# Sorted expert batches of 256 rows, and router logits taken from feature-major data before the normalisation

## The chip, the cores and the metric

The program runs on one core of one Trainium2 chip. The metric is the time on the device in microseconds (us), from the start to the end of one execution, as the median of several. Engines are named as the profile does: PE is TensorE (PEld its weight loads), DVE VectorE, ACT ScalarE, POOL GpSimd, and SP SyncE, which here only issues DMAs.

## The reference, cut to what matters

A graph layer of 3327 nodes with 128 features (attention with three heads over a dense adjacency, two GRU cells) is followed by a mixture of 8 experts of which each node takes two. The part that the change touches:

```python
# x: (3327, 128) result of the graph layer; D = 128, E = 8, K = 2, H = 256
mu = mean(x); var = mean(square(x - mu))
xn = (x - mu) * rsqrt(var + EPS) * gamma + beta       # of an x normalised once before
logits = einsum('bsd,de->bse', xn, Wr) + br
top_vals, top_idx = top_k(logits, 2);  w = softmax(top_vals)
for e in range(8):
    h = gelu(xn @ W1[e] + b1[e])                      # 128 -> 256
    y = y + (h @ W2[e] + b2[e]) * w_full[..., e]      # 256 -> 128
return x + y
```

The graph layer's own last step is `x + de * edge_output + dn * node_output`, with de and dn the diagonal of the adjacency (the same for both).

## The kernel before

Nodes are padded to NP = 3328 = 26 tiles of 128. There are seven chunks of columns, the first of 256 nodes and six of 512. The program has four stages in order of time.

**Graph stage.** Masks, scores and the sum over neighbours for three heads (L1729 on PE, L1242 and L1251 on DVE). The change leaves it alone.

**GRU loop.** One pass for each chunk c. The engines run their own programs and meet by semaphores. PE: `edge(c)` (12 instructions of 512 columns; a matmul of 32-bit floats is two instructions), `attend(c)` (8), `turn_nodes(c-1)` (four transposes), `node(c)` (10). ACT does the gates' sigmoids and tanh, and `attention_kept`. DVE does `candidate` and `mix` for the edge cell, then `nodes_kept(c-1)` (adds the GRU result into `x_kept`, node-major, and takes its statistics), then `candidate` and `mix` for the node cell; the last instruction of the pass raises `dve_mixed`. `temporary(c, 3)` holds the GRU result, feature-major.

Into this loop the dispatch of nodes to experts is woven. The seven chunks make four sets, `SETS = ((0, 1), (2, 3), (4, 5), (6,))`; `due(c, ago)` names the set whose last chunk came `ago` passes earlier. For set g, with the pass in which it runs:

- `deviations(g)` on DVE, ago 1: mean and inverse deviation, 20 small dependent instructions; then `rows_normed(g)` on ACT writes the normalised rows twice (`rows_out`).
- `turn_back(g, k)` on PE and `rows_back(g, k)` on ACT, ago 2: transposes the normalised rows and applies gamma and beta.
- `logits(g)` on PE (L1837, 8 columns for each tile) and `route(g)` on DVE (L1388 to L1406: two maxima, their one-hot forms, running counts), ago 3; `weigh(g)` on ACT; `ranks(g)` on PE (L1845 to L1850), which waits for `route(g)` and stands in PE's program in front of the next `edge`.
- `place(g)` on DVE (L1415 to L1420), ago 4: the slots. Then POOL issues one indirect DMA for each tile and each of the two experts (L611), 128 rows each, into `sorted_dram`, sorted by expert: 52 in all, 12, 16, 16 and 8 by set.

The loop has `BEYOND + 1` = 12 passes. Ahead of the first, DVE waits for `dispatch_in` (L1424), a load that SP issues behind `x_kept`.

**Tables.** DVE works out which expert and which rows each batch has (L1462 to L1497, arrays of 59 batches), then raises `tables_ready`. SP waits for that and for all 52 scatters to have landed.

**Batches.** 59 batches of 128 sorted rows, in a loop written out. For batch n: SP reads two registers, and issues the loads of W1 of the expert (L549) and of the rows (L550) into a ring of 6; DVE masks rows beyond the expert's count (L1504, L1505); PE transposes (L1878, one instruction); ACT applies gamma and beta (L887); PE does two matmuls into the hidden layer (L1887, four instructions), ACT two Gelus (L896), PE two matmuls back (L1899, four instructions), DVE adds b2 (L1514), and POOL issues one indirect DMA (L616) that writes 128 rows to `y_dram` at their nodes. PE's order is `batch_turned(n+3)`, `batch_hidden(n+2)`, `batch_down(n)`; DVE's is `batch_masked(n+4)`, `batch_y(n)`. SP may run up to six batches ahead of `batch_hidden`, and DVE up to six ahead of the landed y.

**Combination.** SP loads `y_dram` in six parts, DVE adds both experts' rows by weight (L1529, 52 instructions), SP writes the result.

## Time and profile before

| | us |
|---|---|
| median of three runs | 1077.2 |
| the three runs | 1083.14, 1077.2, 1075.85 |
| the profiled execution | 1081.5 |
| its span, first to last instruction | 1079.6 |
| PE busy over the span | 900.6 (83%) |
| DVE busy | 719.9 (67%) |
| ACT busy | 633.8 (59%) |
| POOL busy | 133.9 (12%) |
| mean granted clock of PE | 0.911 of full speed |

The page of the profile gives the busy time of each engine, the span in 40 slices, the DMA queues, the chain of work that ended last, the costliest groups and the DMA issues. A share of the whole span says little here, since most of the span is the graph stage. What a change in the last third is worth is read from the views of that third.

### The profile page before, as it was taken

Reading aid. Unit: us, or ns where it says so; the run is one execution under the profiler, and the core shown is the slowest. Engines: PE = TensorE matmul, PEld = TensorE weight load, DVE = VectorE, ACT = ScalarE, POOL = GpSimd, SP = SyncE. Lnnn points to the kernel's source line nnn. Section 1 sums busy time; section 2 is a strip of 40 time slices with the busy share of each in tenths; the row PEclk is TensorE's granted clock in tenths of the full one; section 3 lists DMA queues with packets and bytes.
Section 4 is the critical chain, followed back from the end, with each engine's and each line's share of the span. In section 5 each row is a group of like instructions: output and inputs, shape, how many; then the busy total and the mean of one; then the engine's idle time right before and its main releaser. Section 6 shows DMA issues by size and latency. Waiting matters only on the chain.

```text
span 1079.6 us, 11791 instructions
## 1 busy us (share of the span) xinstructions
PE 900.6 (83%) x2889; PEld 477.1 (44%) x2889; DVE 719.9 (67%) x1385; ACT 633.8 (59%) x968; POOL 133.9 (12%) x174
## 2 busy tenths in 40 slices
PE   5999999996999999999999999998978211778770
PEld 5633343474754344444444444453434201556650
DVE  6433334624998999999999999975767614333335
ACT  0655556413998889989899898962433311444440
POOL 0000000000000000100000100100013563333440
PEclk9999999997999999999999999999989555887785
DMA  9776777021499667454564542213000011333337
GB/s 264 274 253 242 247 251 253 2 95 8 131 305 320 148 168 175 115 131 110 142 191 116 139 110 85 91 38 88 1 5 25 32 47 56 107 111 112 112 100 193
DMA packets 121135, 145.57 MB, mean 135 GB/s; under 512 B 14304, under 2 KB 75778, under 8 KB 120306
## 3 DMA queue, kind: packets, MB, share of 16 engines
q1 hardware_dynamic: 117522, 137.54, 43.6%
q0 software_dynamic: 3552, 7.31, 2.0%
q8 instruction: 26, 0.43, 0.2%
q14 instruction: 35, 0.29, 0.1%
HBM read 122.00 MB, written 22.83 MB: 134 GB/s over the span
## 4 chain that ended last, share of the span: by engine, by line
PE 33%; issue 24%; DVE 19%; SPq 8%; DMA 5%; ACT 4%; DVEq 3%; another core or an unknown queue 2%; POOL 1%; ACTq 0%; POOLq 0%
PE psum L1612 14%; DVE work L1242 9%; PE psum L1729 5%; PE psum L1695 3%; DVE big L1251 3%; DMA big<-adj_cols_dram 2%; SPq L545 2%; SPq L544 2%; SPq L550 2%; SPq L549 2%; DVEq L1242 2%; PE psum L1768 2%; PE psum L1763 1%; PE psum L1764 1%
## 5 line engine op out<-in xcount | busy, mean ns | idle before, releaser
L1729 PE MATMUL psum<-big,h 128*128 128x512 f32 (+1 forms) x1092 | 445.3, 569 | 17.2 <-DVE big L1251 17.1
L1729 PEld LDWEIGHTS psum<-big,h 128*128 128x128 f32 x1092 | 206.7, 192 | 254.8 <-issue 179.3
L1251 DVE TENSOR_TENSOR big<-work,big 128x1536 f32<-128x1536 f32 (+1 forms) x182 | 299.0, 1643 | 9.2 <-ACT work L783 3.6
L781 ACT ACTIVATE work<-work,shift 128x1024 f32<-128x1024 f32 (+1 forms) x182 | 197.9, 1087 | 45.6 <-DVE work L1242 42.7
L1612 PE MATMUL psum<-big,h 128*128 128x512 f32 x312 | 146.3, 612 | 0.0
L1242 DVE TENSOR_SCALAR work<-rows,h 128x512 f32<-128x512 f32 x312 | 137.1, 481 | 3.2 <-POOLq L602 3.2
L783 ACT ACTIVATE work<-work,shift 128x512 f32<-128x512 f32 (+1 forms) x182 | 123.1, 676 | 0.0
L777 ACT ACTIVATE work<-rows,h 128x512 f32<-128x512 f32 x156 | 110.2, 706 | 0.0
L581 POOL TENSOR_SCALAR_AFFINE_SELECT big<-big 128x128 f32<-128x128 f32 x50 | 22.7, 454 | 642.1 <-DMA big<-adj_cols_dram 639.9
L1612 PEld LDWEIGHTS psum<-big,h 128*128 128x128 f32 x312 | 56.6, 191 | 68.8 <-issue 68.3
L655 ACT ACTIVATE work<-big 128x2048 bf16<-128x2048 f32 (+1 forms) x42 | 75.0, 1785 | 2.7
L887 ACT ACTIVATE rows<-psum,u_parts 128x128 f32<-128x128 f32 x59 | 27.0, 458 | 83.4 <-PE psum L1878 81.9
L999 DVE TENSOR_SCALAR rows<-big 128x2048 fp8e4<-128x2048 f32 x36 | 42.5, 1223 | 48.0 <-POOLq L594 47.8
L616 POOL DMA_INDIRECT y_dram<-rows x59 | 57.1, 968 | 93.4 <-DVE rows L1514 91.9
L611 POOL DMA_INDIRECT sorted_dram<-big x52 | 51.8, 996 | 127.2 <-DVE big L1420 112.3
L1878 PE MATMUL psum<-ident,rows 128*128 128x128 f32 x59 | 23.1, 392 | 48.2 <-DVE rows L1505 43.9
L1504 DVE TENSOR_TENSOR rows<-rows 128x129 int32<-128x129 int32 x59 | 17.3, 294 | 60.3 <-DMA rows<-sorted_dram 60.3
L1899 PE MATMUL psum<-rows 128*128 x236 | 50.3, 348 | 7.9 <-DVE rows L1514 7.0
L1887 PE MATMUL psum<-rows 128*128 128x128 f32 x236 | 48.1, 341 | 0.0
L1899 PEld LDWEIGHTS psum<-rows 128*128 128x128 f32 x236 | 40.4, 242 | 14.1 <-issue 14.0
L1514 DVE TENSOR_TENSOR rows<-psum,rows 128x128 f32<-128x128 f32 x59 | 17.2, 292 | 42.4 <-issue 28.5
L896 ACT ACTIVATE rows<-psum,rows 128x128 f32<-128x128 f32 x118 | 37.0, 365 | 11.1 <-PE psum L1887 5.7
(260 smaller groups left out, 765.3 us busy)
## 6 DMA issues: line engine op xcount, KB each, us to landing
big<-adj_cols_dram SPq DMA_DIRECT2D x30, 2048.0 KB, 8.1
sorted_dram<-zeros SPq DMA_DIRECT2D x16, 838.5 KB, 14.4
big<-adj_cols_dram SPq DMA_DIRECT2D x9, 1024.0 KB, 7.0
big<-adj_cols_dram SPq DMA_DIRECT2D x6, 1536.0 KB, 6.5
rows<-w_dram SPq DMA_DIRECT2D x59, 128.0 KB
rows<-stats_dram SPq DMA_DIRECT2D x1, 4608.0 KB, 27.9
rows<-stats_dram SPq DMA_DIRECT2D x1, 3840.0 KB, 20.9
rows<-sorted_dram SPq DMA_DIRECT2D x59, 64.5 KB
```

The lines of the kernel that those rows point to most:

```text
L611: nc.gpsimd.indirect_dma_start(out=sorted_dram[:, :], out_offset=bass.IndirectOffsetOnAxis(ap=slot_at[:, t, k:k + 1], axis=0), in_=rows_ou ...
L616: nc.gpsimd.indirect_dma_start(out=y_dram[:, :], out_offset=bass.IndirectOffsetOnAxis(ap=where_i[:, n:n + 1], axis=0), in_=y_sb[:, n % NY, ...
L655: nc.scalar.activation(unused[:, 0:t1 - t0, 0:w], cols_of(c, t0, t1), ACT.Relu, scale=-1.0, accum_out=negative[:, NQ * c + g:NQ * c + g + ...
L777: nc.scalar.activation(place, row_of(c, LAST), ACT.Relu, bias=h[:, bass.ds(t, 1), H + SCORES + LAST]).then_inc(g_relu, 1)
L781: nc.scalar.activation(both, both, ACT.Exp, bias=shift[:, 0:1], scale=-1.0)
L783: nc.scalar.activation(place, place, ACT.Exp, bias=shift[:, 0:1], scale=-1.0).then_inc(g_e, 1)
L1242: last = nc.vector.tensor_scalar(wexp[:, (n + k) % SLOTS, i, 0:w], row_of(c, i), h[:, bass.ds(t, 1), H + i], 0.0, ALU.subtract, ALU.max)
L1251: nc.vector.tensor_tensor(wadj[:, k % 2, :, 0:w], wexp[:, (n + k) % SLOTS, :, 0:w], ring[:, bass.ds(place, 1), 0:w].broadcast_to([128, HEA ...
L1612: last = nc.tensor.matmul(bank[2 + c % 2][:, 0:w], h[:, t, 0:H], cols_of(c, t, t + 1).squeeze(1), start=t == 0, stop=t == TILES - 1)
L1729: done = nc.tensor.matmul(sums[i], h[:, t, 0:H], wadj[:, t % 2 if v == "plain" else 0, i, 0:w], start=t == 0, stop=t == TILES - 1)
L1887: last = nc.tensor.matmul(bank[2 + n % 3][:, a * 128:(a + 1) * 128], w1_ring[:, n % NX, a * 128:(a + 1) * 128], turned[:, n % 3, :], start ...
L1899: last = nc.tensor.matmul(bank[5 + n % 2][:, 0:H], act_h[:, n % 3, a, :], w2_sb[:, bass.ds(e, 1), a, :].squeeze(1), start=a == 0, stop=a = ...
```

## The change

Two changes in one.

**Batches of 256 rows.** A batch has two sides of 128 rows. `BATCHES` falls from 59 to 33. For each batch SP issues as many DMAs as before, the rows' one twice as large; DVE's two mask instructions and its addition, ACT's one and two activations, and PE's hidden matmuls have twice the columns; PE's transposes and its matmuls back are twice as many, and POOL issues two indirect DMAs for each batch, one a side. W1 is loaded once for each batch.

**Logits from feature-major data.** The normalised rows no longer go back through PE. Since a logit is linear in x, it is the inverse deviation times the product of x with a router whose columns are scaled by gamma and centred (their mean over the features taken away), plus br and the product of beta with Wr. x is the sum of the input, loaded once more feature-major (`x_feat`, into the place of `h`), and the diagonal times the GRU result, `temporary(c, 3)`. So `raw_logits(c)` runs on PE for each chunk two passes after it, on both sources, and `route(g)` forms the logits by four small instructions in place of one. `turn_back`, `rows_back` and `logits` are gone. `route` moves to the head of DVE's pass at ago 2, `ranks` to the end of PE's pass at ago 2, `place` into the same pass of DVE; the loop has 9 passes in place of 12. The wait for `dispatch_in` moves behind the first edge cell, and DVE's `mix` of pass c waits for `raw_logits(c-2)`.

```diff
-BATCHES = 2 * TILES + E - 1
+SIDES = 2
+BATCH = SIDES * 128
+BATCHES = -(-2 * NP // BATCH) + E - 1
...
-        BEYOND = len(CHUNKS) + 4
+        BEYOND = len(CHUNKS) + 1
...
             sp.wait_ge(g_mm, TILES * NCH + FREE)
+            sp.dma_start(x_feat, x_t).then_inc(feat_in, 16)
             sp.dma_start(x_kept, x.rearrange("(t p) f -> p t f", p=128)).then_inc(back_in, 16)
...
-                sp.dma_start(batch[:, n % NX, :], sorted_dram[bass.ds(at, 128), :]).then_inc(b_in[n % NX], 16)
+                sp.dma_start(batch[:, n % NX, :, :], sorted_dram[bass.ds(at, BATCH), :]
+                             .rearrange("(k p) f -> p k f", p=128)).then_inc(b_in[n % NX], 16)
...
                 pool.wait_ge(l_slots, g + 1)
+                pool.wait_ge(n_normed, g + 1)
...
                 pool.wait_ge(b_y, n + 1)
-                nc.gpsimd.indirect_dma_start(
-                    out=y_dram[:, :], out_offset=bass.IndirectOffsetOnAxis(ap=where_i[:, n:n + 1], axis=0),
-                    in_=y_sb[:, n % NY, :], in_offset=None).then_inc(b_out[n % NY], 16)
+                for k in range(SIDES):
+                    nc.gpsimd.indirect_dma_start(
+                        out=y_dram[:, :], out_offset=bass.IndirectOffsetOnAxis(ap=where_i[:, n, k:k + 1], axis=0),
+                        in_=y_sb[:, n % NY, k, :], in_offset=None).then_inc(b_out[n % NY], 16)
...
-                dve.wait_ge(l_psum, g + 1)
+                own, mixed = (bank[2][:, 64 * k:64 * k + nt * E].rearrange("p (t e) -> p t e", e=E) for k in range(2))
+                dve.wait_ge(l_raw, SETS[g][-1] + 1)
                 if g > 0:
                     dve.wait_ge(l_weights, g)
-                order.done(nc.vector.tensor_tensor(logit, bank[2][:, 0:nt * E].rearrange("p (t e) -> p t e", e=E),
-                                                 br_bc.unsqueeze(1).broadcast_to(wide), ALU.add))
+                order.done(nc.vector.tensor_tensor(logit, mixed, diag_of[:, t0:t1].unsqueeze(2).broadcast_to(wide), ALU.mult))
+                order.done(nc.vector.tensor_tensor(logit, logit, own, ALU.add))
+                order.done(nc.vector.tensor_tensor(logit, logit, stats[:, 1, t0:t1].unsqueeze(2).broadcast_to(wide),
+                                                   ALU.mult))
+                order.done(nc.vector.tensor_tensor(logit, logit, br_bc.unsqueeze(1).broadcast_to(wide), ALU.add))
...
             for c in range(BEYOND + 1):
-                if due(c, 4) is not None:
-                    place(due(c, 4))
+                if due(c, 2) is not None:
+                    route(due(c, 2))
                 if c < NCH:
...
                     if c >= 2:
                         dve.wait_ge(n_turned, c - 1)
+                        dve.wait_ge(l_raw, c - 1)
                     mix(c, 1)
+                if c == 0:
+                    centre_router()
+                    dve.wait_ge(dispatch_in_sem, 16)
+                    nc.vector.memset(each_bf, 1.0)
+                    order.done(nc.vector.tensor_copy(upper_bf, upper))
                 if 1 <= c <= NCH:
                     nodes_kept(c - 1)
+                if due(c, 2) is not None:
+                    place(due(c, 2))
                 if due(c, 1) is not None:
                     deviations(due(c, 1))
-                if due(c, 3) is not None:
-                    route(due(c, 3))
...
+            def raw_logits(c):
+
+                c0, w = CHUNKS[c]
+                g = [g for g, chunks in enumerate(SETS) if c in chunks][0]
+                pe.wait_ge(dve_mixed, c + 1)
+                if c == 0:
+                    pe.wait_ge(feat_in, 16)
+                    pe.wait_ge(l_router, 1)
+                if c == SETS[g][0] and g > 0:
+                    pe.wait_ge(l_slots, g)
+                for k, source in enumerate((x_feat[:, c0:c0 + w], temporary(c, 3))):
+                    for t in range(w // 128):
+                        at = 64 * k + E * (c0 // 128 + t - OF_SET[g][0])
+                        last = nc.tensor.matmul(bank[2][:, at:at + E], source[:, 128 * t:128 * (t + 1)], router,
+                                                start=True, stop=True)
+                last.then_inc(l_raw, 1)
...
                 if c < NCH:
                     edge(c)
-                if due(c, 3) is not None:
-                    logits(due(c, 3))
-                    if c >= NCH:
-                        ranks(due(c, 3))
+                if 2 <= c <= NCH + 1:
+                    raw_logits(c - 2)
                 if c < NCH:
                     attend(c)
+                if c == 0:
+                    sum_router()
                 if 1 <= c <= NCH:
                     turn_nodes(c - 1)
-                if due(c, 2) is not None:
-                    turn_back(due(c, 2), 0)
                 if c < NCH:
                     node(c)
                 if due(c, 2) is not None:
-                    turn_back(due(c, 2), 1)
-                if c < NCH and due(c, 3) is not None:
-                    ranks(due(c, 3))
+                    ranks(due(c, 2))
```

## Rows read from the trace of the kernel before

**Rows 1.** By stretch: length, busy PE, PEld, DVE, ACT, POOL (count), clock, DMA share, GB/s

```profile
0.00:723.50 723.50, 689.52 (x2032) 334.83 (x2033) 553.36 (x806) 521.56 (x699) 24.34 (x62) 0.99 0.55 163
...
906.20:1052.90 146.70, 104.01 (x531) 85.94 (x531) 43.91 (x177) 63.90 (x177) 56.19 (x59) 0.79 0.36 107
```

**Rows 2.** The chain that ended last, in order of time: start, us, what

```profile
902.34 2.30 DMA sorted_dram<-big
904.66 0.47 SPq L544
```

**Rows 3.** Timeline of the batch loop: start, us, engine line op, tiles, idle before

```profile
906.20 0.36 SPq L549 DMA_DIRECT2D rows<-w_dram  x1
...
911.60 0.33 SPq L550 DMA_DIRECT2D rows<-sorted_dram  x1
...
913.77 0.33 SPq L550 DMA_DIRECT2D rows<-sorted_dram  x1
...
919.59 0.96 POOL L616 DMA_INDIRECT y_dram<-rows  x1 [16.28 <-DVE rows L1514]
...
1052.86 0.97 POOL L616 DMA_INDIRECT y_dram<-rows  x1 [0.92 <-issue]
```

**Rows 4.** By stretch, as Rows 1: a steady part of the batch loop

```profile
928.00:945.00 17.00, 10.57 (x65) 7.92 (x64) 5.31 (x22) 7.56 (x21) 6.77 (x7) 1.00 0.39 114
```

**Rows 5.** Timeline, POOL's scatter issues: first of set 1, last of 2, first of 3

```profile
846.12 0.97 POOL L611 DMA_INDIRECT sorted_dram<-big  x1 [24.04 <-DVE big L1420]
...
885.65 0.97 POOL L611 DMA_INDIRECT sorted_dram<-big  x1 [0.30 <-issue]
...
892.85 0.96 POOL L611 DMA_INDIRECT sorted_dram<-big  x1 [6.23 <-DVE big L1420]
```

**Rows 6.** Timeline, logits of the last set on PE, and DVE's route of it

```profile
866.66 1.88 PE L1837 MATMUL psum<-u_parts,big 128*128 128x8 f32 x8 [0.87 <-issue]
...
885.64 0.19 DVE L1388 TENSOR_TENSOR big<-psum,u_parts 128x32 f32<-128x32 f32 x1 [21.52 <-remote]
```

**Rows 7.** By stretch, as Rows 1: passes 3 to 6 of the GRU loop

```profile
770.40:844.50 74.10, 53.47 (x165) 26.36 (x164) 53.71 (x164) 26.66 (x50) 12.39 (x12) 0.87 0.03 11
```

**Rows 8.** DVE's waits in passes 3 to 6: us in total, times, longest

```profile
DVE work L1316 <- ACT work L867: 5.6, 3, 2.7
...
DVE work L1316 <- ACT work L873: 1.4, 2, 0.7
...
DVE rows L1316 <- issue: 0.7, 1, 0.7
```

**Rows 9.** Timeline of the GRU loop: ranks, narrow matmuls, route(1), next deviations

```profile
799.18 0.22 PE L1845 MATMUL psum<-big,rows 128*128 128x48 bf16 x1 [7.62 <-DVE big L1406]
...
821.61 1.85 PE L1837 MATMUL psum<-u_parts,big 128*128 128x8 f32 x16
...
834.98 0.22 DVE L1388 TENSOR_TENSOR big<-psum,u_parts 128x64 f32<-128x64 f32 x1
...
839.30 0.16 DVE L1406 TENSOR_TENSOR big<-big 128x8 bf16<-128x8 bf16 x1
...
847.81 0.17 DVE L1343 TENSOR_TENSOR stats<-bn 128x4 f32<-128x4 f32 x1
```

**Rows 10.** The chain: matmuls of 512 columns at full clock, of 128 at half

```profile
753.91 2.59 PE psum L1793 x6
...
974.38 0.87 PE psum L1887 x4
```

**Rows 11.** Timeline, DVE's wait ahead of the first pass

```profile
732.66 0.17 DVE L1424 MEMSET rows<- 128x128 bf16 x1 [7.12 <-DMA rows<-dispatch_dram]
```

**Rows 12.** By stretch, as Rows 1: while the loads ahead of that wait run

```profile
728.00:730.00 2.00, 2.00 (x10) 1.65 (x10) 0.00 (x0) 0.00 (x0) 0.00 (x0) 1.00 1.04 291
```

**Rows 13.** Timeline, first and last instruction of the tables

```profile
892.51 0.15 DVE L1462 COPY rows<-psum 128x8 f32<-128x8 f32 x1
...
903.28 0.65 DVE L1497 TENSOR_REDUCE rows<-rows 128x59 f32<-128x472 f32 x1
```

More of the change, by code:

```diff
@@ L237, in carve @@
             return views
[L240 to L241 removed]
+        (sorted_f, kept_f, logit_f, rest_f, hot1_f, hot2_f, picked_f, hot_f, scan_f, run_f, slot_f, slot_i,
+         w_first, w_second, first, second, where, gap, router, shifted) = carve(
             big[:, 0:(RING + 2 * HEADS) * CHUNK],
[L243 to L244 removed]
+            [TILES * 2 * ROW, NP] + [8 * E] * 5 + [4 * E, 2 * 8 * E, 2 * E // 2]
+            + [2 * TILES] * 4 + [8] * 4 + [E] * 2)
         rows_out = sorted_f.rearrange("p (t k f) -> p t k f", t=TILES, k=2)
         x_kept = kept_f.rearrange("p (t f) -> p t f", f=H)
[L247 removed]
+        x_feat = h[:, :, :].rearrange("p t f -> p (t f)")[:, 0:NP]
         scans = scan_f.bitcast(bf16).rearrange("p (b t e) -> p b t e", b=2, e=E)
@@ L331, in graph_layer_kernel @@
         dve_edge, dve_node, dve_mixed = (sem(n) for n in ("dve_edge", "dve_node", "dve_mixed"))
-        n_turned, n_kept, n_inverse, n_normed, n_back, n_input = (sem(f"n_{n}") for n in (
-            "turned", "kept", "inverse", "normed", "back", "input"))
-        l_psum, l_gap, l_weights, l_hot, l_rank, l_slots = (sem(f"l_{n}") for n in (
-            "psum", "gap", "weights", "hot", "rank", "slots"))
+        n_turned, n_kept, n_inverse, n_normed = (sem(f"n_{n}") for n in ("turned", "kept", "inverse", "normed"))
+        feat_in = sem("feat_in")
+        l_scaled, l_sums, l_router, l_raw, l_gap, l_weights, l_hot, l_rank, l_slots = (sem(f"l_{n}") for n in (
+            "scaled", "sums", "router", "raw", "gap", "weights", "hot", "rank", "slots"))
         sorted_out, tables_ready, sorted_clear, zeros_ready = (sem(n) for n in (
@@ L351, in graph_layer_kernel @@
         LAST_OF = {s[-1]: g for g, s in enumerate(SETS)}
-        def fours(g):
-            t0, t1 = OF_SET[g]
-            return [(t, min(t + 4, t1)) for t in range(t0, t1, 4)]
         def ahead(g):
@@ L361, in ahead @@
             return scans[:, (nt - 1).bit_length() % 2, 7:7 + nt, :]
-        def quads_until(g):
-            return sum(len(fours(k)) for k in range(g))
         def due(c, ago):
             return LAST_OF.get(c - ago) if c >= ago else None
-        BEYOND = len(CHUNKS) + 4
+        BEYOND = len(CHUNKS) + 1
         GROUPS = [(q, range(4 * q, min(4 * q + 4, TILES))) for q in range(-(-TILES // 4))]
@@ L876, in _ @@
                 if due(c, 2) is not None:
[L877 to L879 removed]
+                    weigh(due(c, 2))
             load_table(ACT.Gelu)
@@ L895, in batch_gelu @@
                 for a in range(HALVES):
-                    last = nc.scalar.activation(act_h[:, n % 3, a, :], bank[2 + n % 3][:, a * 128:(a + 1) * 128], ACT.Gelu,
+                    last = nc.scalar.activation(act_h[:, n % 3, a, :], bank[2 + n % 3][:, a * BATCH:(a + 1) * BATCH], ACT.Gelu,
                                                 bias=b1_by[:, n, a:a + 1])
@@ L1877, in batch_turned @@
                     pe.wait_ge(b_input, n - 1)
-                nc.tensor.transpose(bank[n % 2][:, 0:128], batch[:, n % NX, 0:H], ident[:, :]).then_inc(b_turned, 1)
+                for k in range(SIDES):
+                    last = nc.tensor.transpose(bank[n % 2][:, 128 * k:128 * (k + 1)], batch[:, n % NX, k, 0:H], ident[:, :])
+                last.then_inc(b_turned, 1)
             def batch_hidden(n):
@@ L1897, in batch_down @@
                     pe.wait_ge(b_y, n - 1)
-                for a in range(HALVES):
-                    last = nc.tensor.matmul(bank[5 + n % 2][:, 0:H], act_h[:, n % 3, a, :],
-                                            w2_sb[:, bass.ds(e, 1), a, :].squeeze(1), start=a == 0, stop=a == HALVES - 1)
+                for k in range(SIDES):
+                    for a in range(HALVES):
+                        last = nc.tensor.matmul(bank[5 + n % 2][:, H * k:H * (k + 1)], act_h[:, n % 3, a, 128 * k:128 * (k + 1)],
+                                                w2_sb[:, bass.ds(e, 1), a, :].squeeze(1), start=a == 0, stop=a == HALVES - 1)
                 last.then_inc(b_down, 1)
```

124 lines of the change are left out of this document (53 added, 71 removed).

## Prediction

> **What bounds the kernel now.** I read the stretches first, to leave out what the change can't reach. The graph stage takes 723.5 us of the span, with PE at 0.99 of full clock [rows 1]. All else lies in the last 356 us, of which the batch loop is 146.7 [rows 1].
>
> Then the chain of waits, for what joins the stages. The batch loop starts when the last scatter has landed: 2.30 us of DMA up to 904.66, and SP goes on there [rows 2]. The scatter before it is POOL's own work: the first issue of set 1 is at 846.12, the last of set 2, the 32nd, at 885.65, so one takes 39.53 / 31 = 1.275 us, back to back [rows 5]. Then POOL stands idle 6.23 us for the slots of set 3 [rows 5], because DVE began to route that set at 885.64 only, after 21.52 us of idleness, although PE's narrow matmuls end at 868.54 [rows 6]. By the code it can only have waited for their semaphore: it came 17.1 us after them. The view doesn't say why.
>
> Inside the batch loop, the timeline shows SP's issues 2.17 us apart (911.60, 913.77), and 59 y's leave POOL between 919.59 and 1052.86: 133.3 / 58 = 2.30 us each [rows 3]. For one batch of the 59, PE is busy 1.76 us, DVE 0.74, ACT 1.08 and POOL 0.95 [rows 1]: none fills 2.30. So what a batch costs is mainly SP's fixed work for it, two register reads and two issues, whatever the rows.
>
> In passes 3 to 6 of the GRU loop DVE is busy 53.7 of 74.1 us and PE 53.5 [rows 7]: they wait for each other. PE stood 7.62 us at `ranks` for the route [rows 9].
>
> **The change, part by part.** The sum is made on the profiled execution, span 1079.6 and time 1081.5.
>
> *Start of the GRU loop: 0.* DVE now waits 7.12 us for the load of the tables' constants [rows 11]. That wait moves behind the first edge cell, but `x_feat`, 128 x 3328 x 4 = 1.70 MB, goes ahead of it at SP: at 291 GB/s [rows 12] 5.9 us, so the wait ends at about 738.5 in place of 732.66. The node cell of pass 0 then ends near 740, and PE's `attend(1)` needs it then; before it began about 740.6, held by PE's late start. I take 0; bounds are a gain of 1 and a loss of 3, if PE idles and falls to half clock.
>
> *Passes 3 to 6: 7.4 earlier.* DVE's 20.4 us of idleness are 16.6 in named waits (eight groups, 5.6 down to 0.7) and 3.8 of small gaps [rows 7, 8]. The wait for the tanh, 0.7 each [rows 8], stays eight times: 5.6. The others go, since PE no longer stands at `ranks`: the route is done at the head of the pass, and PE's `ranks` comes 9 us later. I keep 2.0 for gates that come late. Two routes gain three small instructions each, at 0.22 and a gap 0.26 us [rows 9]: 1.6. Sum 53.7 + 3.8 + 5.6 + 2.0 + 1.6 = 66.7 in place of 74.1. Can PE follow? A pass is 30 instructions of 512 columns at 2.59 / 6 = 0.43 us [rows 10], 12.9; four transposes of 128 columns, a quarter each, 0.4; and now 16 narrow matmuls, under 1.85 [rows 9]: 15.2 a pass, 60.8 for four, below 66.7. Bounds: 60.8 (PE alone) and 76 (all waits stay).
>
> *Slots of set 2 and scatter: 27.0 earlier at SP.* Pass 6 ends at 837.1. Then come `route(2)`, (839.30 + 0.16 - 834.98) + 0.8 = 5.3, and `nodes_kept` and `place`, which took from 844.5 to 847.81, 3.3 [rows 9]: POOL can start on set 2 near 846. Set 1's slots come in pass 5, some two passes ahead, near 815; its 16 issues of 1.275 end by 836, and would be in time from any start before 825. So POOL works through sets 2 and 3, 24 issues: 846.1 + 23 x 1.275 = 875.4, and 2.3 to land [rows 2] gives 877.7 against 904.66. Cover: set 3's slots are needed at 866.5. Deviations, the weights on ACT, route and place take until about 859 after 846. The tables need at most 903.28 + 0.65 - 892.51 = 11.4 [rows 13], till 870. Both are hidden; if the late semaphore of [rows 6] recurs there, slots come at about 874 and 7 us are lost.
>
> *Filling the batch pipe: 0.7 later.* From SP's first issue to POOL's first y, 906.20 to 919.59, 13.4 us [rows 3]. The same five batches must be in; PE at half clock has 0.22 us for 128 columns [rows 10], twice the columns, and comes near the loads' pace. Bounds 0 and +3.
>
> *The batches: 50.4 earlier.* 33 batches in place of 59. SP keeps its four steps, 2.17 us. DVE and ACT at most double, to 1.5 and 2.2. PE at full clock: two transposes, four instructions of 256 columns, eight of 128, that is 18 times 0.108 = 1.95, and 3.9 at half. POOL has two issues, 2.55: the longest, and it becomes the bound. From first to last y: 65 x 1.275 = 82.9 in place of 133.3. The DMA engines, 0.36 busy at 2.30 us [rows 1], carry less than twice in 2.55: under 0.65. Nothing can make it shorter than POOL's 82.9; upwards it's open, and the rivals price it. The combination after it stays.
>
> Sum: -27.0 + 0.7 - 50.4 = -76.7. The span becomes 1002.9 and this execution's time 1004.8. It was 4.3 above the median of 1077.2, so for the median I say **1001 us**.
>
> [...] Whether PE keeps full clock decides between 1.95 and 3.9. In 928 to 945 it kept full clock with 10.57 of 17 us busy, 62% [rows 4]; over the loop the mean is 0.79 [rows 1]. At POOL's pace it would be busy 1.95 / 2.55 = 76%. So I take full clock. [...]
>
> **The rivals.** *PE's clock.* If it is at half for half of the time, a batch takes 1 / (0.5/3.9 + 0.5/2.55) = 3.08 us in the mean, 17 more over 33: 1018. At half throughout: 1043. For it: 0.79 before. Against: more work in less time.
>
> *POOL's issues stretch or SP's do.* 1.275 was measured with DVE nearly idle. If POOL's took 1.6, 65 x 0.325 = 21 more: 1022; the same if SP's step grew from 2.17 to 3.2 with the larger load. Against: POOL's issues inside the loop before were 0.95 busy in the mean [rows 1], no longer than in the scatter. The Trainium skill, SBUF — State Buffer (SBUF: two separate sides), says that DVE can lock POOL out of the port over which it writes descriptors; these rows show next to nothing of it.
>
> *The batch costs by its rows.* Then 33 of 256 take 2 x 2.30 each, 147 from first to last y, 14 more than before, and only the earlier start is gained, less 0.7: 1065. Against: SP's steps don't scale.
>
> *Slower: late semaphores of narrow matmuls.* One of four groups of narrow matmuls told of its end 17.1 us late [rows 6]. The change has seven, and DVE's `mix` waits for each. Seven late ones cost 120: 1077.2 - 76.7 + 120 = 1120. It decides from the fifth: 5 x 17.1 = 85 against 76.7. Against: the other three groups were in time.
>
> **How the numbers follow.** Forecast 0.73, clock 0.14 (of it 0.02 throughout), stretched issues 0.07, by rows 0.03, late semaphores 0.03. The range reaches from 988 (PE alone sets the loop's pace, 6 less, and the runs' own spread of 7) to 1026 (stretched issues at 1022 with some loss in the fill); it takes in the first, most of the second and the third. A measurement of this kernel can tell about 1% from no change. Faster by over 1% 0.94, within 1% 0.03 (four or five late semaphores), slower 0.03.
>
> **What would show it.** After: 66 y issues on POOL 1.27 us apart, with idle time in front of DVE's b2 addition, and PE near full clock in the loop; SP's wait for the scatter ending near 878; `ranks` with no idle time in front inside the loop; DVE's last GRU instruction near 837. Wrong if POOL waits for DVE in the loop, if its issues are longer than 1.3, if a `mix` waits long for the narrow matmuls, or if the scatter starts set 2 after 853.

## The result, and the profile after

The changed kernel took 1027.4 us (median of 4 runs, 1025.2 to 1031.0) beside 1079.5 for the kernel before (4 runs): 0.952 of it, with a 95% interval of 0.947 to 0.957. The forecast was 1001 with a range up to 1026. The direction was right, the size was not: 26 us are missing. The profiled execution has a span of 1026.9, where the sum had 1002.9.

The first view of the changed kernel's trace is the timeline. Columns: start and duration in us, engine, line, operation, output and input; in brackets the idle time before and what ended it. It shows the last GRU instruction on DVE, the scatter's start and end on POOL (L611), the first load of SP, and the first and the last y (L617).

```profile
833.76 0.69 DVE L1453 TENSOR_TENSOR work<-work 128x512 f32<-128x512 f32 x1
...
845.87 0.97 POOL L611 DMA_INDIRECT sorted_dram<-big  x1 [10.04 <-DVE big L1411]
...
875.16 0.96 POOL L611 DMA_INDIRECT sorted_dram<-big  x1 [0.30 <-issue]
...
880.05 0.36 SPq L547 DMA_DIRECT2D rows<-w_dram  x1
...
894.86 0.96 POOL L617 DMA_INDIRECT y_dram<-rows  x1 [18.74 <-DVE rows L1527]
...
1000.36 0.97 POOL L617 DMA_INDIRECT y_dram<-rows  x1 [0.30 <-issue]
```

Up to the first y nearly all came as worked out. The GRU loop ends at 834.5 (837.1 was forecast, 844.5 before [rows 7]). POOL starts set 2 at 845.87 (846.1) and goes through its 24 issues without a gap to 875.16 (875.4), where before it had stood for 6.23 us [rows 5]. The first y leaves at 894.86 (the forecast was 877.7 + 1.5 for SP's start [rows 2, 3] + 14.1 = 893.3). But from the first y to the last it takes 105.5 us where the sum had 82.9. These 22.6 us are nearly the whole miss; the span is 24.0 longer than the sum, and the first y was 1.6 late.

The same view of POOL, a few batches later, shows what the stream looks like:

```profile
901.55 0.96 POOL L617 DMA_INDIRECT y_dram<-rows  x1 [1.91 <-DVE rows L1527]
902.81 0.96 POOL L617 DMA_INDIRECT y_dram<-rows  x1 [0.30 <-issue]
904.08 0.97 POOL L617 DMA_INDIRECT y_dram<-rows  x1 [0.31 <-issue]
...
906.62 0.97 POOL L617 DMA_INDIRECT y_dram<-rows  x1 [0.30 <-issue]
907.90 0.97 POOL L617 DMA_INDIRECT y_dram<-rows  x1 [0.30 <-issue]
911.13 0.97 POOL L617 DMA_INDIRECT y_dram<-rows  x1 [2.27 <-DVE rows L1527]
```

An issue takes what it took before, 0.97 us, and 1.27 from one to the next [rows 5]. They come in bursts of two to eight, and then POOL waits for y's. The chain of waits through the burst from 901.55 runs through SP's queue. Columns: start, duration, and SP's queue by line, or "issue", time in which nothing that the profile shows is waited for.

```profile
903.77 0.52 issue
904.38 0.66 SPq L548
905.06 0.71 SPq L542
905.81 0.72 issue
906.53 0.71 SPq L543
907.26 0.71 SPq L543
908.01 0.70 SPq L546
908.72 0.72 issue
909.43 0.70 SPq L547
910.33 0.83 SPq L548
```

From 903.8 to 910.2, that is from just before POOL's third issue until 1.3 us after the end of its sixth, SP gets on only in strides of about 0.7 us. Six of its small steps take 662 to 729 ns, three times nothing is recorded for 0.5 to 0.7 us, and the nine steps between take 3 to 21 ns, less than elsewhere. The raw record of SP's queue for the end of this stretch (start in us, duration in ns, operation, line):

```
907.26 714 SEQ_ASSERT      L543
907.99 729 EVENT_SEMAPHORE L546
909.44 700 FUSED_REGOPS    L547
910.19  42 FUSED_REGOPS    L548
910.27  29 MOVE            L548
```

In the batch at 903.4 the same check of L543 took 18 ns, the same wait 17 ns and the same register operation 42. So two batches' loads of W1 lie 2.2 us apart outside such a stretch, and 5.87 across it (904.30 to 910.17). In the loop before, where POOL sent one y in 2.30 us, SP's issues lay 2.17 us apart [rows 3], and of its steps only a few DMA issues took 0.65 us or more, no register step, move or check.

PE does not look like the cause. Over 895 to 1001 its granted clock is 0.89 with 72.56 of 106 us busy, where the clock was 0.79 before [rows 1]:

```profile
core 0: us, PE busy (x) PEld busy (x) DVE busy (x) ACT busy (x) POOL busy (x), PEclk, DMA share, GB/s
...
895.00:1001.00 106.00, 72.56 (x427) 62.94 (x425) 29.66 (x88) 39.63 (x88) 64.21 (x66) 0.89 0.38 108
```

The combination after the last y takes 26.5 us, as before.

### The profile page after: what moved, and what is told of

Same layout as the page of the kernel before. It is cut to its first block, busy times and chain, and to the rows that moved or that the text cites. A ratio compares the mean times of both kernels' runs of the same rounds, so it can differ in the third digit from the quotient of the medians.

```text
span 1026.9 us, 10850 instructions
## 1 busy us (share of the span) xinstructions
PE 875.1 (85%) x2850; PEld 461.3 (45%) x2850; DVE 709.7 (69%) x1323; ACT 609.8 (59%) x883; POOL 142.4 (14%) x181
## 4 chain that ended last, share of the span: by engine, by line
PE 32%; issue 26%; DVE 22%; SPq 7%; DMA 4%; ACT 4%; DVEq 3%; POOL 1%; another core or an unknown queue 1%; ACTq 0%; POOLq 0%
PE psum L1626 15%; DVE work L1229 9%; PE psum L1743 5%; PE psum L1709 4%; DVE big L1238 3%; DMA big<-adj_cols_dram 2%; SPq L548 2%; DVEq L1229 2%; SPq L542 2%; SPq L543 1%; DVE big L1543 1%; PE psum L1609 1%; PE psum L1807 1%; ACT work L785 1%; SPq L547 1%
## 5 line engine op out<-in xcount | busy, mean ns | idle before, releaser
L783 ACT ACTIVATE work<-work,shift 128x1024 f32<-128x1024 f32 (+1 forms) x182 | 197.8, 1087 | 46.1 <-DVE work L1229 43.0
L617 POOL DMA_INDIRECT y_dram<-rows x66 | 64.7, 980 | 60.5 <-DVE rows L1527 45.8
L611 POOL DMA_INDIRECT sorted_dram<-big x52 | 52.4, 1008 | 99.8 <-DVE big L1411 84.9
L1891 PE MATMUL psum<-ident,rows 128*128 128x128 f32 x66 | 15.8, 326 | 54.8 <-DVE rows L1518 43.6
L874 ACT ACTIVATE work<-psum,u_parts 128x256 f32<-128x256 f32 x33 | 18.6, 564 | 64.3 <-PE psum L1891 48.5
L1527 DVE TENSOR_TENSOR rows<-psum,rows 128x256 f32<-128x256 f32 x33 | 14.0, 425 | 46.4 <-PE psum L1914 33.0
L973 DVE TENSOR_TENSOR work<-work,psum 32x512 f32<-32x512 f32 (+1 forms) x7 | 4.5, 637 | 58.0 <-ACT work L672 58.0
L883 ACT ACTIVATE work<-psum,rows 128x256 f32<-128x256 f32 x66 | 27.6, 471 | 25.3 <-PE psum L1901 15.5
L1516 DVE TENSOR_TENSOR rows<-rows 128x258 int32<-128x258 int32 x33 | 14.1, 427 | 36.8 <-DMA rows<-sorted_dram 35.1
L1901 PE MATMUL psum<-work,rows 128*128 128x256 f32 x132 | 39.2, 425 | 0.0
L1914 PEld LDWEIGHTS psum<-rows,work 128*128 128x128 f32 x264 | 37.0, 207 | 4.6 <-issue 2.3
```

Source lines behind the costliest of these rows:

```text
L611: nc.gpsimd.indirect_dma_start(out=sorted_dram[:, :], out_offset=bass.IndirectOffsetOnAxis(ap=slot_at[:, t, k:k + 1], axis=0), in_=rows_ou ...
L617: nc.gpsimd.indirect_dma_start(out=y_dram[:, :], out_offset=bass.IndirectOffsetOnAxis(ap=where_i[:, n, k:k + 1], axis=0), in_=y_sb[:, n % ...
L783: nc.scalar.activation(both, both, ACT.Exp, bias=shift[:, 0:1], scale=-1.0)
```

## The experiments

Three theories stood after this reading. **A:** while POOL issues indirect DMAs back to back, the other engines are held up. **B:** SP's row load of 256 rows is what delays SP. **C:** PE, by its clock or its throughput. The runs went to five chips, and that proved to matter. The kernel before, timed on each of them, tells two kinds apart: on chips 1, 2 and 8 it took 1073.1, 1073.7 and 1071.2 us (all runs 1069.7 to 1076.8), on chips 3 and 12 1079.8, 1080.5 and 1083.4 (1073.8 to 1086.2). The first are called quiet here, the second disturbed. The pair of the result, at 1079.5, looks like the disturbed kind; on which chip it ran isn't recorded. Chip 12 was used at two times and was disturbed at both; the others were used once each, so for them "a kind of chip" could also be a state of the chip at that time.

All runs in one table; "stream" is from the first to the last y on POOL in the profiled execution, and "slow steps" are SP's register reads, register operations, moves and checks after 870 us that last 0.65 to 0.80 us.

```
kernel                    chip   us      of before [95%]         stream  slow steps
the change (the result)   ?      1027.4  0.952 [0.947, 0.957]    105.5   25
the change, again         2      1003.3  0.934 [0.931, 0.936]     83.5    0
the change, again         3      1025.9  0.950 [0.946, 0.954]    102.2   22
one y per batch           1       992.2  0.924 [0.923, 0.926]     74.3    0
one y per batch           8       989.6  0.925 [0.922, 0.927]     72.8    0
one y per batch           12      996.2  0.924 [0.920, 0.927]     72.8    0
before, each y twice      1      1087.1  1.014 [1.012, 1.017]    149.1    0
before, each y twice      8      1089.9  1.017 [1.015, 1.019]    149.6    0
before, each y twice      12     1136.9  1.050 [1.047, 1.053]    185.9   45
W1 from ACT's queue       1       998.6  0.931 [0.930, 0.933]     84.0    0
W1 from ACT's queue       3      1019.6  0.944 [0.939, 0.948]    101.6   13
rows from ACT's queue     2      1000.5  0.932 [0.930, 0.935]     83.9    0
W1 from ACT, more reads   2      1003.9  0.934 [0.932, 0.937]     83.9    0
pause of two memsets      8      1024.4  0.956 [0.954, 0.958]    105.5    0
pause of two memsets      12     1029.4  0.954 [0.951, 0.958]    106.0    9
W1 from ACT, one memset   12     1024.7  0.945 [0.941, 0.949]    104.4    0
router part alone         1      1050.0  0.978 [0.976, 0.980]    133.0    0
batch part alone          2      1027.6  0.956 [0.953, 0.958]     84.2    0
```

### One y issue per batch

```diff
-                for k in range(SIDES):
+                for k in range(1):
                     nc.gpsimd.indirect_dma_start(
```

> The changed kernel, but POOL sends only side 0 of each batch's y (33 issues in place of 66), and the combination reads rows of the sorted array in place of y (same sizes), so the outputs lack the expert part. Changed kernel: first to last y 105.5 us, 3.2 per batch, with stretches in which each of SP's instructions takes about 0.70 us in place of 0.02 to 0.3. Theory A (POOL's back-to-back indirect DMAs slow SP's instructions): no slow stretches, SP sets the pace with its undisturbed 2.23 us, 32 x 2.23 = 71 us from first to last y, time 1028 - 34 = 994. Theory B (SP's row load, now 256 rows, is itself slow or held back): the slow stretches stay, 105 us, 1027. Theory C (PE: clock or throughput): unchanged, 105 us, 1027.

This kernel leaves out half of the y's, so its output lacks the experts' part. Measured on chip 1: 992.2 us and SP's steps undisturbed, as theory A had it. At the time this seemed to refute B and C. It did not, since the changed kernel itself has no slow steps on this kind of chip, which the next runs showed. The same kernel twice more:

> One y issue per batch again (the combination reads other rows, outputs lack the expert part), in the hope of a chip on which engines are held up: there before takes some 1080 us and the changed kernel 1026. Theory A (while POOL issues indirect DMAs back to back, the other engines' waits and instructions are held up, on such a chip): with one issue per batch POOL has no bursts in the loop, nothing is held, 71 to 75 us from first to last y, some 0.925 of before, less only what the scatter's burst costs (about 5 us). Theory B (the 256-row load on SP is what fails on such a chip): 3.2 us per batch, 0.955. On an undisturbed chip: 992 again.

Chip 8, quiet again: 0.925, nothing decided.

> One y issue per batch (the combination reads other rows, outputs lack the expert part). Undisturbed chip: 0.924 and about 72 us from first to last y, as twice before. Chip with the hold-ups: theory A (POOL's back-to-back issues hold the others up): the loop has no bursts, 71 to 75 us, SP without instructions of 0.70 us, 0.925 to 0.93. Theory B (SP's 256-row load): 100 us or more, 0.95.

Chip 12 was disturbed, and this run decides: 0.924, with SP's loads of 256 rows as they are and at full pace. The timeline of SP's queue shows 2.25 us from one batch's loads to the next:

```profile
921.86 0.33 SPq L547 DMA_DIRECT2D rows<-w_dram  x1
922.38 0.38 SPq L548 DMA_DIRECT2D rows<-sorted_dram  x1
924.11 0.33 SPq L547 DMA_DIRECT2D rows<-w_dram  x1
924.63 0.38 SPq L548 DMA_DIRECT2D rows<-sorted_dram  x1
```

So the large load by itself is not slow, and theory B falls. PE did the batches' whole work there in 72 us, 64.08 of them busy, at full clock (1.00). By itself that would not clear the clock, which was lower in the changed kernel. Two traces of the changed kernel do: from 893 to 976 the result's has a granted clock of 0.94 and 50 y issues, the one of chip 2 below 0.95 and 65, though its first y is only 2.0 us earlier. At the same clock the y's still fall behind, so C falls too.

### The kernel before, with each y sent twice

```diff
+                for to in (y_dram, again_dram):
                     nc.gpsimd.indirect_dma_start(
-                        out=y_dram[:, :], ...
+                        out=to[:, :], ...
```

> The kernel before, with the y of each batch sent twice: the second indirect DMA goes to another array that nobody reads. SP's loads stay at 128 rows. POOL alone needs 117 x 1.275 = 149 us from first to last y in place of 133.3. Theory A (POOL's dense issues slow SP): SP shows instructions of about 0.7 us and the loop goes at about the changed kernel's 3.2 us a batch, 58 x 3.2 = 186 us, time 1081 + 53 = 1134. Theories B (the larger row load) and C (PE): only POOL's own 149 us, 1097.

Chip 1: 1.014, the stream 149.1 us, which is POOL's 117 issues of 1.275 and no more. Theory A as first put, that dense issues slow SP on any chip, was wrong: 118 issues stand close and SP has no slow step. Repeated on chip 8 (expectation in the same words, and the result too: 1.017, 149.6 us):

> Every y of the kernel before sent twice, again. Theory A on a chip with the hold-ups: POOL's 118 issues come in bursts of 2 to 8 and the loop takes 1.6 us per issue as in the changed kernel there, 117 x 1.6 = 187 us, 1.04 to 1.05 of before. Theory B: 149 us, 1.014 as on the undisturbed chip. On an undisturbed chip: 1.014 either way.

> Every y of the kernel before sent twice, with SP's loads at 128 rows. Undisturbed chip: 149 us from first to last y, 1.014 to 1.017, as twice before. Chip with the hold-ups: theory A (dense issues alone bring them) some 1.6 us per issue, 117 x 1.6 = 187 us, 1.05. Theory B' (they need the 256-row load on top): 149 us, 1.015.

Chip 12: 1.050 and 185.9 us, where A had 1.05 and 187. With SP's loads at 128 rows, and none of the change in it, dense y issues bring the slow steps (45), the bursts (six issues, then two, again and again) and 1.6 us per issue. PE's granted clock was 0.63 in this stretch where it was 0.84 on chip 1, but PE was busy for only 115 of 187 us; what the lower clock adds to the hold-up was not measured apart. The waits on other engines show the hold-up too, before the loop. Timeline of this kernel on chip 12, rows of PE, DVE and POOL:

```profile
868.14 1.87 PE L1838 MATMUL psum<-u_parts,big 128*128 128x8 f32 x8 [1.27 <-ACT big L852]
...
886.94 0.19 DVE L1389 TENSOR_TENSOR big<-psum,u_parts 128x32 f32<-128x32 f32 x1 [21.30 <-remote]
...
886.97 0.97 POOL L611 DMA_INDIRECT sorted_dram<-big  x1 [0.30 <-issue]
894.15 0.97 POOL L611 DMA_INDIRECT sorted_dram<-big  x1 [6.21 <-DVE big L1421]
```

The same two groups on chip 1:

```profile
861.27 1.87 PE L1838 MATMUL psum<-u_parts,big 128*128 128x8 f32 x8 [0.87 <-ACT big L852]
...
863.18 0.19 DVE L1389 TENSOR_TENSOR big<-psum,u_parts 128x32 f32<-128x32 f32 x1 [4.01 <-PE psum L1838]
```

On chip 1 DVE goes on 0.04 us after PE's eight narrow matmuls, with POOL in the middle of its burst. On chip 12 they are over by 870.0, and DVE goes on at 886.94, in the moment in which POOL begins the last issue of its burst of 32. In the first trace of the kernel before it was 885.64 and 885.65 [rows 5, 6]. The trace also records when a semaphore rises: PE's rises at 863.16 on chip 1, but at 886.91 on chip 12 and at 885.62 in the first trace, so it is late already on PE's side. The burst alone isn't enough: on chip 12 DVE went on in time at 859.19 behind the narrow matmuls of the set before, with ten issues of the same burst out. On quiet chips POOL has all 40 issues of this scatter in one run (841.17 to 891.17 on chip 1) and no gap of 6 us. So what the prediction called the late semaphore of narrow matmuls goes with POOL's burst on a disturbed chip, not with the matmuls.

### The change again

> The changed kernel as it is, once more, beside the others. The two runs of before and after the change showed SP instructions of 0.70 us, the four experiments since showed none, so it has to be seen whether they come again. If they belong to the changed kernel (SP with two issues per batch, one of them of 256 rows, under a dense POOL): again 3.2 us per batch, 105 us from first to last y, some 0.952 of before. If they belonged to the chip or the state in which that run was made: 2.55 us per batch, 83 to 85 us, some 0.932 of before.

Chip 2: 1003.3 us, 0.934. The stream takes 83.5 us where the forecast had 82.9. Timeline of POOL, its first and last y there:

```profile
892.86 0.97 POOL L617 DMA_INDIRECT y_dram<-rows  x1 [19.56 <-DVE rows L1527]
...
976.32 0.97 POOL L617 DMA_INDIRECT y_dram<-rows  x1 [0.31 <-issue]
```

Against this, the groups of instructions over the stream of both kinds of trace, first that of the result, then chip 2 (columns: busy time, mean ns of one, idle time before them and who ended it):

```profile
L617 POOL DMA_INDIRECT y_dram<-rows x66 | 64.7, 980 | 60.5 <-DVE rows L1527 45.8 <-issue 14.8
```

```profile
L617 POOL DMA_INDIRECT y_dram<-rows x66 | 64.6, 979 | 39.4 <-DVE rows L1527 21.1 <-issue 18.3
```

POOL's own 66 issues are equal. Of the idle time behind DVE's addition 18.74 and 19.56 us lie before the first y. Inside the stream that leaves 27.1 us for the result and 1.5 on chip 2: POOL lacks y's in the one and not in the other.

The hold-up also shows ahead of the loop. DVE's table arithmetic (its first instruction is L1467 here) takes 8.9 us on chip 2, 855.12 to 864.02. In the result's trace, under POOL's burst of 24, it takes 18.9, 857.92 to 876.82: the steps follow each other in 0.2 us up to 858.7, where POOL has its 11th issue, and later many of them lie 0.7 us or more apart. It ended 0.7 us after the last issue had, before a scatter lands (2.30 us [rows 2]), so it cost the kernel little: SP's first load came 4.9 us after the last scatter issue, 3.8 on chip 2.

> The changed kernel again, to find whether the 0.70 us instructions of SP, which the first pair of traces shows and seven later ones don't, come back. Chip or state: either 3.2 us per batch with SP instructions of 0.70 us (about 0.952 of before, 1025 us) or 1.284 us per y issue, 83.5 from first to last (0.934, 1003 us). If the two groups of earlier runs differ by chance within one chip, something between them.

Chip 3: 1025.9 us, 0.950, 102.2 us in the stream, 22 slow steps. Each of the two results of the change was seen with a kernel before of its own kind (1073.7 and 1079.8 us), and within a chip the four runs of the change differ by 2.6 us at most, so the difference isn't chance.

### Which queue carries the loads

```diff
-                e = sp.value_load(expert_i[0:1, n:n + 1], ...)
-                sp.dma_start(w1_ring[:, n % NX, :], w1[bass.ds(e, 1), :, :].squeeze(0)).then_inc(b_in[n % NX], 16)
+            def load_w1(n):          # on ACT, eight batches ahead
+                e = act.value_load(expert_i[0:1, n:n + 1], ...)
+                act.dma_start(w1_ring[:, n % NX, :], w1[bass.ds(e, 1), :, :].squeeze(0)).then_inc(b_in[n % NX], 16)
```

> The changed kernel with the W1 load of each batch (a register read and a DMA issue) moved from SP's queue to ACT's. Theory A with SP as the only victim: SP's instructions per batch are halved, even at 0.7 us each they fit in 9 x 0.7 = 6.3 us only while POOL bursts, and the mean falls to POOL's 2.55: 83 us from first to last y, time 1005. Theory A with every queue slowed alike: ACT shows instructions of 0.7 us too and the gain is halved, about 95 us, 1017. Theory B: SP still issues the large load, but saves one issue of two: 95 to 105 us. Theory C: 105 us, 1027.

Chip 1: 998.6 us. The stream is POOL's 84.0; it is no faster than that of the change on a quiet chip, so SP was never the limit there. The gain over the change comes earlier: from POOL's last scatter issue to the first y 14.4 us (870.20 to 884.61) in place of 20.5 (872.34 to 892.86). ACT has loaded the first six W1 before the scatter has landed (862.69 to 868.05), and SP's first six row loads then take 6.3 us (873.49 to 879.80) in place of 12.8 (876.72 to 889.50).

> W1 from ACT's queue, beside as_changed_b on the same chip. If SP is undisturbed: 84.0 us from first to last y, 0.931. If SP is disturbed: SP has half of its instructions, so that about 9 x 0.7 = 6.3 us of a disturbed batch in place of 12.6; the loop would lose 6 to 11 us in place of 22, 1005 to 1010 us, or nothing if two reads less keep it ahead of POOL.

Chip 3: 0.944 beside the change's 0.950. The expectation of 1005 to 1010 was wrong, 101.6 us in the stream and 1019.6. Relieving SP leaves the stream as it was, so SP isn't the only one that is held up. Timeline of PE, DVE and POOL:

```profile
920.16 0.42 DVE L1536 TENSOR_TENSOR rows<-psum,rows 128x256 f32<-128x256 f32 x1 [1.48 <-PE psum L1923]
920.24 1.05 PE L1923 MATMUL psum<-rows,work 128*128 x8
...
922.81 0.97 POOL L614 DMA_INDIRECT y_dram<-rows  x1 [0.31 <-issue]
...
925.39 0.42 DVE L1536 TENSOR_TENSOR rows<-psum,rows 128x256 f32<-128x256 f32 x1 [4.27 <-PE psum L1923]
...
926.09 0.97 POOL L614 DMA_INDIRECT y_dram<-rows  x1 [2.31 <-DVE rows L1536]
```

PE's matmuls of 920.24 end at 921.29, and DVE adds b2 to their result at 925.39 only, 4.1 us late, 1.6 after POOL's sixth issue has ended (923.78). POOL then waits for just this addition. The pattern repeats every 9.6 us: six issues, three batches, and 3.28 us from the sixth to the next, 2.31 of them idle for the late y. That is 3.2 us per batch, about the pace of the change on such chips, however SP's work is divided.

> The changed kernel with the row load of each batch (a register read and the issue of 256 rows) moved from SP's queue to ACT's; W1 stays at SP. If two issues per batch on one queue are what slows SP, either move frees it: 84 us from first to last y as with W1 at ACT (84.0), 0.931 of before. If it is the 256-row load that is slow wherever it stands: ACT is delayed in its place, 95 us or more, 0.942.

> W1 from ACT's queue as in w1_from_act, but SP reads two more registers per batch and has the second wait back, so that its undisturbed time per batch is again 3 x 0.57 + 0.52 = 2.23 us and it executes as many instructions as in the changed kernel, with one DMA issue in place of two. If the number of SP's instructions is what starves it: 0.70 us instructions come back, 3.2 per batch, 105 us. If it is the second DMA issue: 84 us as in w1_from_act. If SP's 2.23 alone, with nothing slowed, left too little slack under POOL's 2.55: 84 to 88 us.

Both ran on chip 2. 83.9 us in the stream for each, at 1000.5 and 1003.9 us. They were to explain slow steps that don't occur on a quiet chip, so they say nothing of the cause. `sp_reads` gives one useful number: with 2.22 to 2.29 us from one row load to the next while the ring fills, SP stays ahead of POOL's 2.55 and costs the stream nothing.

### A pause on POOL

```diff
                         in_=y_sb[:, n % NY, k, :], in_offset=None).then_inc(b_out[n % NY], 16)
+                for _ in range(2):
+                    order.done(nc.gpsimd.memset(zeros[:, :], 0.0))
```

> The changed kernel with two small memsets on POOL (0.21 us each, with their waits some 0.5 us together) behind the two y issues of each batch. Undisturbed chip: POOL's 2.55 becomes about 3.05 to 3.2 per batch, 98 to 103 us from first to last y, 1018 to 1022. Chip with the hold-ups, theory A with the back-to-back issues as cause: the pause ends each burst after two issues, nothing is held, 98 to 103 us again, so no slower or even faster than the changed kernel there (105). If a pause of 0.5 us does not end a burst: the pauses come on top, 105 + 16 = 120 us, 1042.

Chip 8, quiet: 3.23 us per batch, 105.5 in the stream, 1024.4. The pause costs its full 0.68 us per batch, more than the 0.5 expected (98 to 103 us).

> Two memsets with their waits behind the two y issues of each batch. Undisturbed chip: 3.23 us per batch, 0.956, as before. Chip with the hold-ups, theory A: bursts of two never reach the third issue, behind which the hold-ups began in the traces of the changed kernel, so the loop keeps its 3.23 us per batch, 106 us, and SP, DVE and ACT show no late waits: 0.955, nearly the changed kernel's own time there (0.950 to 0.952). If a pause of that size does not end them: the pauses come on top, 120 us or more, 0.965 to 0.97.

Chip 12, disturbed: 106.0 us in the stream and 0.954. Timeline of POOL:

```profile
930.16 0.98 POOL L617 DMA_INDIRECT y_dram<-rows  x1 [0.50 <-POOL zeros L621]
931.44 0.97 POOL L617 DMA_INDIRECT y_dram<-rows  x1 [0.30 <-issue]
932.40 0.49 POOL L621 MEMSET zeros<- 128x129 f32 x2
933.40 0.98 POOL L617 DMA_INDIRECT y_dram<-rows  x1 [0.50 <-issue]
```

POOL never waits for a y inside the stream here, and the pause comes nearly free: the kernel has the pace of one with the hold-ups (102 to 105) and of one with the pause on a quiet chip (105.5). The change as it is was not run on chip 12. One point of the expectation was wrong: SP still shows 9 slow steps, so pairs of issues do touch it, but too briefly to starve POOL.

```diff
+                order.done(nc.gpsimd.memset(zeros[:, :], 0.0))      # on top of W1 from ACT's queue
```

> W1 from ACT's queue, and one small memset with its wait behind the two y issues of each batch, where pool_gaps had two (3.23 us per batch). Undisturbed chip: 2.55 + about 0.4 = 2.95 us per batch, 97 us from first to last y, some 13 more than w1_from_act, 0.943. Chip with the hold-ups: if the short pause still ends the bursts, the same 97 us, 0.939 to 0.943; if not, w1_from_act's 3.19 per batch there plus the pause, 112 to 118 us, 0.955.

Chip 12: 104.4 us, between the two expectations (97, and 112 to 118). Timeline of POOL:

```profile
916.09 0.97 POOL L614 DMA_INDIRECT y_dram<-rows  x1 [0.28 <-POOL zeros L617]
917.36 0.97 POOL L614 DMA_INDIRECT y_dram<-rows  x1 [0.31 <-issue]
918.33 0.22 POOL L617 MEMSET zeros<- 128x129 f32 x1
918.83 0.97 POOL L614 DMA_INDIRECT y_dram<-rows  x1 [0.28 <-issue]
...
923.31 0.97 POOL L614 DMA_INDIRECT y_dram<-rows  x1 [2.02 <-DVE rows L1537]
```

From one batch's first issue to the next's it is 2.74 us in place of 2.55: the memset fills most of a gap that stands there anyway, and the pause is 0.2 us and not the 0.4 expected. The bursts go on over it, six or eight issues and then some 2 us of waiting for a y. So 0.2 us per batch does not end them, and 0.68 does.

### The two parts alone

The router part alone is the change with `SIDES = 1` (59 batches of 128 rows), the batch part alone the kernel before with the hunks that name `SIDES` and `BATCH`.

> Only the router part of the change: batches stay at 128 rows, 59 of them. By the prediction's steps SP's wait for the scatter ends 27.0 us earlier and the batch loop keeps its 133.3 us: time 1079.5 - 27 = 1052. If the narrow matmuls or the earlier scatter disturb more than the trace of the changed kernel shows, less than 27.

Chip 1: 0.978, 23.1 us less; the stream takes 133.0 us as before [rows 3].

> Only the batch part of the change: 256-row batches with the router as before. The router part alone gave 0.978 of before (23 us). If the parts add up: the whole less 23 us, so 0.974 of before with the loop at 3.2 us per batch, or 0.953 with the loop at 2.55. The first y comes some 14 us after the scatter has landed, the loop then takes 105 or 84 us.

Chip 2: 0.956, 46.1 us less; the scatter ends at 897.35 on POOL, 23.5 later than in the router part alone (873.84). The two parts add up to 69.2 us, and the whole gives 70.3 on chip 2.

### The best version

Of the versions that compute everything, W1 from ACT's queue has the lowest times, 998.6 us on chip 1 and 1019.6 on chip 3, and beats the kernel before on both kinds of chip. Against the change it is shown on chip 3 only: 1017.2 to 1022.5 us beside 1024.8 to 1026.9 (0.944 and 0.950 of before, with intervals that overlap a little). On quiet chips the two ran on different ones (0.931 and 0.934), and the intervals overlap.

## Why the prediction was right and wrong, point by point

**Start of the GRU loop, 0; passes 3 to 6, 7.4 earlier.** Right in sum. The loop ended at 834.5 where 837.1 was forecast. The waits in front of `ranks` are gone, as said, and DVE stands idle in its named waits for only 6.7 us in the stretch from 760 to 834, where the sum had 5.6 and 2.0 for passes 3 to 6.

**Set 2 and scatter, 27.0 earlier.** Right on the result's own trace: the last scatter issue is at 875.16 against 875.4. (The forecast's own terms, 837.1 + 5.3 + 3.3, give 845.7 where it went on with 846.1; POOL started at 845.87.) The tables were taken to be done by 870; the hold-up stretched them to 876.8, and SP's first load came at 880.05 where 877.7 + 1.5 was forecast. But 6.2 of the 27.0 were a gain only beside that trace of before. Its gap of 6.23 us [rows 5] came from the hold-up. On a quiet chip the kernel before has no such gap, and the router part gains 23.1.

**Filling, 0.7 later.** 14.8 us from SP's first issue to the first y, 14.1 forecast. On chip 2 it is 16.7 (876.15 to 892.86), inside the stated bounds. There the whole span, 1002.9, is the forecast's to the tenth, and that is partly luck: the scatter's last issue is 3.1 us earlier than forecast (872.34), the filling 2.6 longer.

**The batches, 82.9 us from first to last y.** This is the term that failed: 105.5. Its mechanism, that POOL becomes the bound at 65 x 1.275, is right on quiet chips (83.5). The sum took this floor itself as the time and so let the other engines keep up with POOL. In the result's trace they don't: POOL stands idle for 27.1 us behind DVE's additions inside the stream. On a disturbed chip the bound itself, POOL without a pause, brings the delays of the others that then starve it. The step behind it that was wrong is the reading of the 17.1 us [rows 6]. It was put down to narrow matmuls, priced as a rival against their seven groups, and thought absent from a loop without them. The rows had the better condition in sight: the wait ended as POOL began the last of 32 issues, to 0.01 us [rows 5, 6]. The change makes POOL's issues dense through the whole loop. Why some chips show the hold-up and others don't was not to be seen in any row.

**The rival "POOL's issues stretch or SP's do"** (chance 0.07, 1022) is the one that came nearest, by its second half: SP's step grows from 2.17 to about 3.3 us in the mean. Its reason was wrong, since SP's larger load takes 0.38 us to issue in place of 0.33, and `one_y_c` runs it at 2.25 us per batch. POOL's issues hardly stretched, 980 ns in the mean on the result and 979 on chip 2, beside 968 in the loop before. (The forecast read 0.95 there because its window ends inside the last of the 59 issues.) The Trainium skill, SBUF — State Buffer (SBUF: two separate sides), has DVE locking POOL out of a port that the two share; these 12 ns are all that the rows could show of it. By the same section of the Trainium skill POOL can lock DVE out too, but PE and ACT never wait on anyone at these ports. What the runs show is wider: on disturbed chips PE's semaphore came 17 us late and SP's steps took 0.7 us, which that rule does not explain.

**PE's clock** (0.14) did not come. In the stream on chip 2 PE is busy 64.27 of 83 us, 77% where 76% was forecast, at 0.95 of full clock:

```profile
893.00:976.00 83.00, 64.27 (x429) 56.43 (x427) 29.22 (x87) 41.02 (x88) 63.49 (x65) 0.95 0.47 136
```

In the result's own stream the clock is 0.89, but the y's fall behind there at 0.94 too (893 to 976), so the 22.6 us are not the clock's. The forecast that the clock would be nearly full, with short waits between the groups of matmuls, was right on chip 2. The Trainium skill, TensorE: Matmul & The Clock Gate (Loop structure matters more than you think), has PE go cold where a long DMA wait stands between every two matmuls; here PE idled for only 18.7 of 83 us in all, so no run of this case tests that rule.

**Batch by its rows** (0.03) and **late semaphores as a loss of 120 us** (0.03) did not come. The range's upper end of 1026 was drawn from the stretched issues and is 1.4 us short of the result. It was too narrow for a rival of the right size with a chance that was set too low. One chance was also put in the wrong place: 1065, "by its rows", is 1.1% under 1077.2, so "faster by over 1%" should have been 0.97 and not 0.94.

## What to carry to other kernels

Before an engine is taken as the new bound, look at what the trace shows around its densest stretches: a wait elsewhere that ends in the very moment in which POOL's burst of indirect DMAs ends may be a price of the burst, not of the work that was waited for. A change that fills POOL's queue is to be priced both ways, at POOL's pace and at that of the held-up loop (here 2.55 and 3.2 us per batch). And a time from one chip is one sample: the same two kernels stood at 0.934 on one chip and 0.950 on another.

## What the runs showed of the hardware

- On two of five chips (3 and 12), and most likely on that of the result, POOL's indirect DMAs of 128 rows in a dense row (1.27 us apart) go with a hold-up of the other engines. SP gets on in strides of about 0.7 us: a check of 18 ns took 714, a register operation of 42 ns took 700. Waits of DVE end up to 4.1 us late in the loop, and one ended 17 us late in a burst of 32.
- When it sets in differs. In the loop it was near the third issue of a burst of six (903.8 in the burst from 901.55). In the bursts ahead of the loop DVE still kept its pace at the tenth or eleventh issue (859.19 on chip 12, 858.7 in the result's trace). In the loop it ended 1.3 to 1.6 us after the end of the last issue, in the two bursts of 32 as the last issue began.
- It needs neither large loads nor the batches of 256: the kernel before with doubled y issues has it on chip 12 (185.9 us in place of 149.1 on chip 1).
- One issue in 2.2 us did no harm on chips 1, 8 and 12 (74.3, 72.8 and 72.8 us), and a pause of 0.68 us behind every second issue was enough to keep POOL fed on chip 12; one of 0.2 us was not.
- What differs between the chips stays open, and so does the path. No run parts POOL's issuing from the writes of the DMAs that it starts, since both grow and shrink together in all of them.
